# Routing the class token in the opening, and a new order of work on all engines, in a one-core image tower on Trainium2

## The chip, the core and the metric

The kernel runs on one core of one Trainium2 chip. The core has five engines with queues of their own: TensorE (PE: matrix products and transposes, its weight loads shown as PEld), VectorE (DVE), ScalarE (ACT), GpSimd (POOL) and SyncE (SP, which here only issues DMAs). They work in parallel and wait for each other on semaphores. The metric is the device time of one execution in microseconds (us). All data is fp32; `fp32r` is an fp32 format of TensorE with fewer bits, so a product that must be exact is made of three: high by high, high by low and low by high.

## What is computed

For each of 16 images of 256 tokens with 256 features: an attention-free mixing of tokens with a residual and a layer norm; one class token in front; a gated linear recurrence over the 257 tokens, added; and a mixture of experts (one shared, eight routed, the two best for each token), added. Cut to what matters:

```python
q, k, v = proj(Wq, bq), proj(Wk, bk), proj(Wv, bv)          # x: (16, 64, 256, 4)
ek = exp(k)
num, den = einsum('ts,nsd->ntd', ew, ek * v), einsum('ts,nsd->ntd', ew, ek)
h = layernorm((sigmoid(q) * num / den) @ out_w + out_b + flatten(x)) * ln_g + ln_b
h = concatenate([cls_tok of each image, h], axis=1)
u = layernorm(h)
r, i = sigmoid(u @ W_r + b_r), sigmoid(u @ W_i + b_i)
a = sigmoid(log_a) * r
hs = scan(h_s = a_s * h_{s-1} + (1 - a_s) * i_s * (u @ W_in + b_in)_s)
h = h + hs @ W_out + b_out
v = layernorm(h)
gate = top 2 of softmax(v @ Wr), scaled to sum 1
h = h + gelu(v @ Wfc_s + b) @ Wproj_s + b + sum_e gate_e * (gelu(v @ Wfc[e] + b) @ Wproj[e] + b)
```

The recurrence starts from zero with the class token, which is the same for all images. So its row is the same in all 16 outputs and is computed once.

## The kernel before

**Stages.** `mixer_tensor`, `mixer_scalar`, `mixer_vector`, `mixer_pool` and `mixer_sync` hold the program of the engines for the first stages; `experts_tensor` and its likes hold the rest. The mixer is a pipeline over 16 images with four in flight. In step t the projection and the sums over tokens work on image t, the layer norm, gates and recurrence on image t-1, its output and the second norm on image t-2, and routing and the shared expert on image t-3. Steps 0 to 3 are the opening, steps 4 to 15 a loop of pairs (`step`, twice), steps 16 to 18 the drain. Then come the eight routed experts, in blocks of 256 rows taken from per-expert lists `v_rows` in DRAM.

**Who sets the order.** Each engine's order is written out by hand as a list of calls with (t, parity). The calls with the same meaning on different engines meet through semaphores. Below, `name[n]` is the call's work on image n. On TensorE: `project0/1` (fp32 projection, L832), `sums0/1` (numerators and denominators, L925), `turn_y`, `turn_u`, `turn_v` (transposes, L839, all through the one buffer `ps_t`), `h_out` (L913), `gates0/1` and `input0/1` (split products, L748), `attention` (L898), `logits` (L994), `rank` (L879 to L883), `hidden` 0 to 7 (split product of the shared expert's first layer, L748) and `ffn_out` 0 to 7 (second layer, L764). On ScalarE: `exp0/1`, `copy_yt`, `copy_u`, `copy_v` (copies out of `ps_t`), `tanh0/1`, `gelu_j`, `high` (high half of the activation, L1293) and `share` (the tanh that gives the two scores' shares). On VectorE: `ekv0/1` (E, L1765), `ratio0/1` (reciprocal and product, L1772), `y_last` (L1864), `h_sum` (L1785 and statistics), `h_norm`, `u_stats`, `u_norm`, `u_low`, `gate_a` and `gate_b` (decay, recurrence input and scan, L1858), `v_sum`, `v_norm`, `v_low`, `low` (low half, L1593), `best` and `second` (the two best experts by small operations of 128x16, each waiting for the one before), `places` and `slots_out` (row numbers in the lists), `base_sum` (shared output plus residual, L1996 and L1999). On GpSimd: `rstd_h`, `rstd_u`, `rstd_v` (L517, L520), `affine` (L585, L587), `out_bias` (L598), `rows_out` (four scatters, L524), and the splits `low_first`, `low_second`, `next_low_first`, `next_low_second` of expert weights (L510, two instructions of 128x1024 each) and `next_weights` (six DMAs).

**The class token.** It goes through the mixer in the opening in `cls_` calls. Its routing stands in the drain: `cls_logits` (`cls_c` on TensorE: 8 small matmuls that turn the row into columns, then 4 for the logits), `cls_high` and `cls_share` on ScalarE, `cls_route` (`cls_c` on VectorE, 28 counted operations in a chain), `cls_d` (its count into `run`, the number of rows in each expert's list so far) and `cls_out` (two scatters). `run` is shared: what reads `ps_h` or `run` waits for `run_ready`, which also counts the class token from image 14 on. `CLS_AFTER`, `past_cls` say where it stands.

**Start of the experts.** After the drain TensorE makes the class token's shared output (24 matmuls, L1257), loads the eight ends of the experts' blocks from `bounds` into registers (`block_limits`, L1269), runs 8 matmuls with no use for their result (`WARM`, L1262), and transposes the first 256 rows (L1234). ScalarE and VectorE make `xh` and `xl` from them (L1572, L2246), for which the first hidden product waits.

## Time and profile before

| | |
|---|---|
| Median of 3 runs | 1000.52 us (1000.45 to 1001.65) |
| The profiled execution | 1000.1 us, its span 998.5 us |
| Mean granted clock of TensorE | 0.971 |
| Busy: TensorE, its weight loads | 941.2 us (94%), 879.6 us (88%) |
| Busy: VectorE, ScalarE, GpSimd | 676.5 us (68%), 458.8 us (46%), 380.1 us (38%) |
| DMA | 84.84 MB, mean 85 GB/s |

The time is the whole execution; the span runs from the first to the last instruction. Busy time of an engine is not work at its best rate: matmuls are pipelined, and TensorE's clock is granted at 2.4 GHz or at half of that. A view by stretches tells both: its columns are the stretch, its length, and for each engine the busy time with the number of instructions, then the granted clock, the DMA share and the rate. A view of waits names for whom an engine stood idle. In a timeline each row has its start, how long it took, the engine, the line, the operation, out<-in with shapes, the number of merged instructions, and in brackets the idle time before it and what ended it.

### The profile page before, as it was taken

The numbers are of one execution on the slowest core, as the hardware profiler recorded it, in microseconds if no ns is written. First come the engines' busy times: TensorE is split into PE (matmuls) and PEld (weight loads), VectorE is DVE, ScalarE is ACT, GpSimd is POOL, SyncE is SP. The second block draws the span as 40 slices with busy tenths as digits, with TensorE's granted clock in tenths as the row PEclk, the third lists the DMA queues.
The fourth block names the chain that finished last, engine by engine and source line by source line (L and its number), as shares of the span: only waits on it lengthen the run. The fifth ranks groups of instructions, "written<-read, shape, count | busy, mean of one in ns | idle before, by whom it ended". The sixth has DMA issues, their size and how long they took to land.

```text
span 998.5 us, 21487 instructions
## 1 busy us (share of the span) xinstructions
PE 941.2 (94%) x6801; PEld 879.6 (88%) x6801; DVE 676.5 (68%) x2092; ACT 458.8 (46%) x1132; POOL 380.1 (38%) x470
## 2 busy tenths in 40 slices
PE   6879999999999999999886999999999999999996
PEld 4667898888898888988786999999999999999995
DVE  3687878877888777788887365645656456554643
ACT  2214344444444434444332455555555555555553
POOL 5272533334324243233535334342423435342322
PEclk9989999999999999999999899999999999999998
DMA  9305111011110011100025727372463826474222
GB/s 271 134 18 168 43 43 37 17 32 42 42 42 16 26 42 42 42 21 11 33 95 195 202 47 204 55 216 43 101 157 50 215 47 145 117 174 92 43 43 32
DMA packets 49187, 84.84 MB, mean 85 GB/s; under 512 B 6415, under 2 KB 30881, under 8 KB 49154
## 3 DMA queue, kind: packets, MB, share of 16 engines
q0 software_dynamic: 31056, 57.46, 23.6%
q1 hardware_dynamic: 18098, 26.96, 9.2%
q8 instruction: 17, 0.28, 0.1%
q14 instruction: 16, 0.13, 0.0%
HBM read 55.34 MB, written 29.09 MB: 85 GB/s over the span
## 4 chain that ended last, share of the span: by engine, by line
PE 59%; issue 21%; POOL 9%; DVE 7%; ACT 1%; POOLq 1%; DMA 0%; DVEq 0%; SPq 0%; ACTq 0%
PE ps_nd L764 17%; PE ps_proj L748 13%; PE ps_ri L748 6%; PE ps_nd L925 6%; PE ps_proj L832 5%; POOL out L709 5%; PE ps_ip L748 4%; PE ps_h L913 2%; PE ps_t L839 2%; PE ps_ip L898 2%; PE ps_t L1234 1%; POOL v_rows L524 1%; DVE E L1765 1%; POOL rstd L520 1%; DVE yb L1999 1%
## 5 line engine op out<-in xcount | busy, mean ns | idle before, releaser
L1593 DVE TENSOR_TENSOR GL<-g_act,GH 128x256 fp32r<-128x256 f32 (+1 forms) x416 | 171.3, 425 | 166.4 <-ACT GH L1293 164.9
L1288 ACT ACTIVATE g_act<-ps_proj,fcb 128x256 f32<-128x256 f32 (+1 forms) x272 | 129.5, 476 | 277.9 <-PE ps_proj L748 253.4
L764 PE MATMUL ps_nd<-w2h,GH 128*128 128x256 f32 x832 | 240.6, 289 | 2.4 <-DVE GL L1593 2.2
L764 PE MATMUL ps_nd<-w2h,GL 128*128 128x256 f32 x832 | 233.8, 281 | 0.0
L764 PE MATMUL ps_nd<-w2l,GH 128*128 128x256 f32 x832 | 232.9, 280 | 0.0
L764 PEld LDWEIGHTS ps_nd<-w2h,GH 128*128 128x128 f32 x832 | 156.3, 188 | 6.9 <-issue 1.8
L1293 ACT CAST GH<-g_act 128x256 fp32r<-128x256 f32 (+1 forms) x416 | 161.0, 401 | 1.1
L764 PEld LDWEIGHTS ps_nd<-w2l,GH 128*128 128x128 f32 x832 | 157.0, 189 | 0.0
L764 PEld LDWEIGHTS ps_nd<-w2h,GL 128*128 128x128 f32 x832 | 156.4, 188 | 0.0
L748 PE MATMUL ps_proj<-xh,w1h 128*128 128x256 f32 (+1 forms) x544 | 126.8, 315 | 10.1 <-DVE E L1765 8.7
L709 POOL DMA_INDIRECT out<-yb,rows_to x72 | 115.6, 1605 | 16.7 <-issue 14.0
L748 PE MATMUL ps_proj<-xl,w1h 128*128 128x256 f32 (+1 forms) x544 | 111.8, 287 | 0.0
L748 PE MATMUL ps_proj<-xh,w1l 128*128 128x256 f32 (+1 forms) x544 | 111.3, 286 | 0.0
L748 PEld LDWEIGHTS ps_proj<-xh,w1h 128*128 128x128 f32 x544 | 86.7, 192 | 26.1 <-issue 14.3
L338 POOL TENSOR_TENSOR carrier_pool<-minus_half 1x1 f32<-1x1 f32 x48 | 10.9, 226 | 206.4 <-DVE slots L1987 113.9
L748 PEld LDWEIGHTS ps_proj<-xl,w1h 128*128 128x128 f32 x544 | 86.6, 194 | 0.0
L748 PEld LDWEIGHTS ps_proj<-xh,w1l 128*128 128x128 f32 x544 | 85.9, 193 | 0.0
L524 POOL DMA_INDIRECT v_rows<-v,slots x64 | 67.9, 1060 | 32.7 <-issue 16.6
L832 PE MATMUL ps_proj<-wproj,x 65*128 65x256 f32 x256 | 71.2, 425 | 6.8 <-DMA x<-x 6.2
L925 PE MATMUL ps_nd<-E,ewT 128*128 128x512 f32 x128 | 72.8, 702 | 2.8 <-DVE E L1765 2.8
L832 PEld LDWEIGHTS ps_proj<-wproj,x 65*128 65x128 f32 x256 | 64.1, 327 | 9.9 <-issue 7.9
L338 POOL TENSOR_TENSOR carrier_y<-minus_half 1x1 f32<-1x1 f32 x36 | 9.4, 261 | 162.8 <-DVE yb L2314 162.8
(266 smaller groups left out, 1829.9 us busy)
## 6 DMA issues: line engine op xcount, KB each, us to landing
R<-v_rows SPq DMA_DIRECT2D x37, 260.0 KB, 2.7
w1h<-fc_w POOLq DMA_DIRECT2D x9, 1024.0 KB
w2h<-pj_w POOLq DMA_DIRECT2D x9, 1024.0 KB
stage<-fc_w POOLq DMA_DIRECT2D x9, 1024.0 KB, 11.4
stage<-pj_w POOLq DMA_DIRECT2D x9, 1024.0 KB, 13.9
v_rows<-tail_rows SPq DMA_DIRECT2D x8, 520.0 KB, 4.5
x<-x SPq DMA_DIRECT2D x16, 256.0 KB, 3.5
out<-yb SPq DMA_DIRECT2D x16, 256.0 KB, 2.1
```

The costliest lines, as they stand in the source:

```text
L338: return pool.tensor_tensor(carrier[use][:], half, half, ALU.add)
L524: pool.indirect_dma_start(out=v_rows, out_offset=bass.IndirectOffsetOnAxis(ap=where_to, axis=0), in_=source, in_offset=None).then_inc(sema ...
L709: pool.indirect_dma_start(out=out, out_offset=bass.IndirectOffsetOnAxis(ap=rows_to[:, a:a + 1], axis=0), in_=yb[:, a, :], in_offset=None, ...
L748: last = pe.matmul(dst, w[a][:, k, cols], rhs, start=(q == 0), stop=(q == len(parts) - 1))
L764: last = pe.matmul(banks[a], g[:, j, a * P:(a + 1) * P], w[i][:, j, :], start=(j == 0 and q == 0), stop=(j == HT - 1 and q == 2))
L832: last = pe.matmul(ps_proj[:, h, :], head_view(par, lt, h), wproj[:, h, :], start=True, stop=True)
L839: last = pe.transpose(ps_t[:, f, lt * P:(lt + 1) * P], src[:, lt, f * P:(f + 1) * P], ident[:])
L898: last = pe.matmul(ps_ip[:, lt, :], HS[:, k, lt * P:(lt + 1) * P], wout_sb[:, k, :], start=(k == 0), stop=(k == FT - 1))
L925: last = pe.matmul(ps_nd[:, tt, :], ewT[:, s, tt * P:(tt + 1) * P], E[:, s, :], start=(s == 0), stop=(s == LT - 1))
L1288: act.activation(g_act[:, j % G_SLOTS, 0:width], banks[j % len(banks)][:, 0:width], ACT.Gelu_apprx_tanh, bias=fcb[i][:, j:j + 1]).then_inc ...
L1293: act.copy(GH[:, j, 0:width], g_act[:, j % G_SLOTS, 0:width]).then_inc(gh_done, 1)
L1593: dve.tensor_tensor(GL[:, j, 0:width], g_act[:, j % G_SLOTS, 0:width], GH[:, j, 0:width].bitcast(F32), ALU.subtract).then_inc(gl_done, 1)
```

## The change

**Class token.** `CLS_AFTER` goes from image 14 to 0: it is routed before image 0. Its calls are cut finer (`cls_cols`, `cls_logits`, `cls_count` on TensorE; `cls_halves`, `cls_route`, `cls_places`, `cls_run` on VectorE) and stand in the opening; the two scatters end GpSimd's opening. From there on all waits on `run_ready` and on the routing chain count it.

**Order.** The lists of TensorE, ScalarE, VectorE and GpSimd are new in the opening and the drain, and those of TensorE, ScalarE and VectorE in the loop's step. `low_first` moves ahead of `rstd_h[0]`, `low_second` ahead of the class token's rstd and `rstd_h[1]`, `next_weights` behind `rstd_v[1]`, `next_low_second` ahead of `rows_out[14]`. The projection and all other operations are what they were.

**Limits.** TensorE loads five limits (`AHEAD = 6`), transposes the first rows and then loads the other three; the 8 warm-up matmuls go. ScalarE loads its eight as before.

The core of the diff; in the lists only the step's are given whole, as they are after:

```diff
-        CLS_AFTER = NIMG - 2
-        CLS_STEP = CLS_AFTER + 2
+        CLS_AFTER = 0
         def past_cls(n, count):
-            return count if isinstance(n, int) and n >= CLS_AFTER else 0
+            return 0 if isinstance(n, int) and n < CLS_AFTER - 1 else count
...
             def cls_c():
                 pe.wait_ge(cls_dve, 9)
-                pe.wait_ge(run_ready, CLS_AFTER)
+                pe.wait_ge(hx_done, CLS_AFTER + 2)
                 columns(CV, ps_h[:, 0, :], 2).then_inc(cls_pe, 1)
+            def cls_scores():
...
             def logits(t, par):
                 if live(t - 3):
                     n = t - 3
-                    if isinstance(n, int) and n == CLS_AFTER:
-                        cls_d()
...
-            limits = block_limits(pe)
-            for _ in range(WARM):
-                pe.matmul(ps_t[:, 0, :], ones_r[:], W2H[0][:, 0, :], start=True, stop=True)
+            limits = [0] + block_limits(pe, 1, AHEAD)
             transpose_rows(0)
+            limits += block_limits(pe, AHEAD, NE + 1)
             pe.wait_ge(b_done, FT * NIMG)
...
+            def cls_rows():
+                count, chain = cls_chain(CLS_MASK)
                 dve.wait_ge(route_act, CLS_AFTER + 1)
-                dve.wait_ge(run_ready, CLS_AFTER)
-                dve.wait_ge(slots_ready, CLS_AFTER)
```

The steps of the loop, before and after:

```
TensorE before: turn_y project0 h_out attention project1 logits hidden0 sums0 hidden1 sums1 hidden2
  hidden3 turn_u hidden4 rank hidden5 gates0 turn_v hidden6 input0 gates1 input1 ffn_out0 ffn_out1
  hidden7 ffn_out2 ... ffn_out7
TensorE after:  turn_y project0 h_out attention project1 logits hidden0 hidden1 sums0 hidden2 hidden3
  hidden4 hidden5 turn_u hidden6 sums1 hidden7 gates0 input0 rank turn_v gates1 ffn_out0 ... ffn_out7
  input1
VectorE before: ekv0 h_sum h_norm ekv1 v_sum best u_stats second u_norm ratio0 u_low v_norm low0 low1
  ratio1 y_last low2 places low3 low4 low5 low6 slots_out v_low gate_a low7 gate_b base_sum
VectorE after:  ekv0 h_sum h_norm ekv1 v_sum best u_stats v_norm low0 u_norm low1 ratio0 u_low low2
  second low3 ratio1 y_last low4 places slots_out v_low low5 low6 low7 gate_a base_sum gate_b
```

The pieces of the opening and the drain of which the prediction speaks, after the change:

```
TensorE, opening: ... turn_u[1] cls_logits project1[3] turn_v[0] gates0[1] hidden0[0] turn_y[2] input0[1]
  cls_count h_out[2] hidden1[0] logits[0] ...
ScalarE, opening: ... copy_u[1] exp1[3] cls_share copy_v[0] copy_yt[2] gelu_j0[0] ...
VectorE, opening: ... u_low[1] v_norm[0] cls_route ekv1[3] v_low[0] y_last[2] cls_places cls_run h_sum[2]
  best[0] ...
GpSimd, opening:  low_first rstd_h[0] affine[0] rstd_u[0] out_bias[0] low_second cls_rstd rstd_h[1]
  affine[1] rstd_u[1] out_bias[1] rstd_v[0] rstd_h[2] affine[2] rstd_u[2] rstd_v[1] next_weights
  rows_out[0] out_bias[2] cls_out
TensorE, drain:   turn_y[15] hidden0[13] h_out[15] hidden1[13] attention[14] logits[13] ... ffn_out2[13]
  turn_u[15] ffn_out3[13] ... ffn_out7[13] hidden0[14] hidden1[14] logits[14] attention[15] ...
  hidden4[15] rank[15] ffn_out0[15] ...
VectorE, drain:   ... places[14] slots_out[14] base_sum[14] best[15] second[15] low0[15] places[15] ...
```

## Rows read from the trace of the kernel before

**Rows 1.** Busy time by stage: opening, loop, drain with experts' start, experts.
```profile
0.00:106.50 106.50, 85.31 (x415) 67.55 (x416) 70.54 (x175) 29.08 (x74) 46.49 (x69) 0.94 0.48 138
106.50:476.90 370.40, 361.69 (x2342) 325.71 (x2341) 298.67 (x970) 166.80 (x384) 136.98 (x173) 0.97 0.10 34
476.90:553.80 76.90, 59.91 (x449) 56.19 (x447) 59.93 (x211) 24.15 (x62) 32.63 (x30) 0.94 0.29 101
553.80:998.50 444.70, 434.31 (x3600) 430.11 (x3600) 247.39 (x740) 238.74 (x612) 163.95 (x199) 0.99 0.49 111
```

**Rows 2.** Timeline of TensorE: hidden0 of three steps in a row.
```profile
179.53 0.38 PE L748 MATMUL ps_proj<-xh,w1h 128*128 128x256 f32 x1 [0.68 <-DVE E L1765]
...
209.41 0.39 PE L748 MATMUL ps_proj<-xh,w1h 128*128 128x256 f32 x1 [0.68 <-DVE E L1765]
...
240.91 0.39 PE L748 MATMUL ps_proj<-xh,w1h 128*128 128x256 f32 x1 [0.68 <-DVE E L1765]
```

**Rows 3.** Waits of TensorE in the drain: total us, times, longest.
```profile
PE ps_h L994 <- DVE run L1761: 3.2, 1, 3.2
PE ps_h L994 <- issue: 2.7, 1, 2.7
PE ps_nd L764 <- DVE GL L1593: 1.6, 1, 1.6
...
PE ps_t L839 <- DVE U L1616: 1.0, 1, 1.0
```

**Rows 4.** Timeline in the drain: class token's columns, its chain's first and last operation.
```profile
498.11 1.05 PE L777 MATMUL ps_h<-ones_pp,CV 1*128 1x1 f32 x8
...
499.39 0.16 DVE L1724 TENSOR_TENSOR xl<-ps_h,xh 128x4 fp32r<-128x4 f32 x1
...
505.88 0.17 DVE L1756 CAST c_slots<-rslot 128x2 uint32<-128x2 f32 x1
```

**Rows 5.** Drain timeline of GpSimd and VectorE; then yb's durations (min/median/max ns).
```profile
477.62 4.67 POOL L510 TENSOR_TENSOR w1l<-stage,w1h 128x1024 fp32r<-128x1024 f32 x2
...
478.05 4.81 DVE L1999 TENSOR_TENSOR yb<-yb,h 128x512 f32<-128x512 f32 x1
...
L1999 DVE TENSOR_TENSOR yb<-yb,h x16: 691/691/5261, 110.1 to 541.0; 128x512 f32<-128x512 f32 x16
```

**Rows 6.** Loads of the limits by line (ns); then the timeline around them.
```profile
L1269 PEldq TENSOR_LOAD <-bounds x8: 295/308/724, 543.4 to 548.8; - x8
...
548.63 0.17 DVE L2241 COPY info<-R 128x8 f32<-128x8 f32 x1 [2.41 <-DMA R<-v_rows]
...
551.32 1.05 PE L1234 MATMUL ps_t<-ident,R 128*128 128x128 f32 x4
```

**Rows 7.** Busy time in a stretch at the experts' start, with the granted clock.
```profile
547.60:557.90 10.30, 7.05 (x31) 6.66 (x32) 2.12 (x9) 1.83 (x4) 0.37 (x2) 0.50 0.14 40
```

**Rows 8.** Opening: a weight load's issue and us to landing, rstd_h[0], v_norm[0].
```profile
15.20 0.96 POOL L486 DMA_DIRECT2D stage<-pj_w  x1
...
stage<-pj_w POOLq DMA_DIRECT2D x1, 1024.0 KB, 13.3
...
31.25 0.20 POOL L517 TENSOR_TENSOR ve<-mv,eps 128x2 f32<-128x2 f32 x1 [9.65 <-DVE mv L1613]
...
67.45 3.67 DVE L1616 TENSOR_SCALAR v<-h,mv,rstd 128x256 f32<-128x256 f32 x2
```

**Rows 9.** A step: chain pieces of sums and hidden; U, out_bias and turn_u.
```profile
457.39 1.72 PE ps_nd L925 x4
459.11 0.71 PE ps_proj L748 x6
...
184.85 0.73 DVE L1616 TENSOR_SCALAR U<-h,mv,rstd 128x256 f32<-128x256 f32 x2
185.66 1.28 POOL L598 TENSOR_TENSOR h<-h,bout_bc 128x512 f32<-128x512 f32 x1 [0.86 <-DVE U L1616]
185.90 0.27 PE L839 MATMUL ps_t<-ident,U 128*128 128x128 f32 x1
```

More of the change, by code:

```diff
@@ L1183, in mixer_tensor @@
             ffn_out(17, 1, 1)
+            turn_v(17, 1)
+            ffn_out(17, 1, 2)
+            hidden(17, 1, 7)
+            ffn_out(17, 1, 3)
             input0(17, 1)
[L1185 to L1196 removed]
@@ L2154, in mixer_vector @@
[L2154 to L2167 removed]
+            ratio0(17, 1)
+            v_low(16, 0)
+            low(16, 0, 7)
+            gate_a(16, 0)
+            gate_b(16, 0)
@@ new lines, in mixer_vector @@
+            base_sum(16, 0)
+            ratio1(17, 1)
+            y_last(17, 1)
+            low(17, 1, 0)
+            v_sum(17, 1)
+            best(17, 1)
+            low(17, 1, 1)
+            v_norm(17, 1)
+            gate_a(17, 1)
+            low(17, 1, 2)
+            h_sum(18, 0)
+            low(17, 1, 3)
+            ekv0(16, 0)
+            ratio0(18, 0)
+            v_sum(18, 0)
+            low(17, 1, 4)
+            second(17, 1)
+            h_norm(18, 0)
+            ekv1(16, 0)
```

512 lines of the change are left out of this document (251 added, 261 removed).

## The prediction

> **What bounds the kernel now.** I read three views in this order: the busy time by stage, what TensorE waited for in each stage, and then the timeline at the places where it waited. The stages say most [rows 1]: in the loop TensorE is busy 361.7 of 370.4 us and in the experts 434.3 of 444.7, so those two stages, 815 of 998.5 us, can hardly change. The opening (images filling the pipeline, 106.5 us) has 21.2 us in which TensorE is idle, the drain with the start of the experts (76.9 us) has 17.0. VectorE is busy 59.9 of these 76.9 us and 70.5 of 106.5, with long chains of small dependent operations between. So the change can win only in 183 us, and there what decides is when VectorE and GpSimd finish the item for which TensorE waits.
>
> In the loop each step has one idle piece of 0.68 us, in front of the first hidden product, which waits for the last E of the next image [rows 2]. Steps take 29.88 and 31.50 us in turn (from 179.53 to 209.41, then to 240.91): the longer ones hold a stretch at the lower clock. Nothing in the edit touches the chain project1, three ScalarE operations, E, on which the 0.68 us hang.
>
> **The drain, order and class token.** Its waits are in [rows 3]: 3.2 us until the class token's count is in `run`, 2.7 in front of the logits of image 13, 1.6 for GL and 1.0 for U.
> - Class token away: the 3.2 us are a pure wait, logits[14] behind `cls_d`, behind the VectorE chain that runs from 499.39 to 506.05 [rows 4]. The chain is 6.7 us long, of which about 6.0 busy. It goes, and so does its TensorE part (14 matmuls, some 1.5 us by the 1.05 us of eight of them [rows 4]). What is late next: hidden0[14] now stands first in that step and waits for v_low[14], which the new VectorE order has behind places and slots of image 13. I lay it out with the measured durations and find no stall there, because the 6.0 us that VectorE saves lie just before. Sum: -3.2 -1.5 = -4.7.
> - The 2.7 us: VectorE's yb sum, 0.69 us in the median, took 4.81 us because GpSimd ran its two weight splits (2.35 us each) at that time [rows 5]. The new step puts base_sum ahead of gate_b, so the sum now just escapes and the two scans of gate_b, with both inputs in SBUF, meet the splits. attention[14], moved ahead of logits[13], waits for these scans. I find the same stall, 0.8 us longer: +0.8.
> - The 1.6 us for GL have the same cause, a second 5.26 us yb sum [rows 5] beside the other half of the splits. That half moves ahead of image 14's sum: -1.6. The U wait: turn_u[15] goes behind three ffn parts: -1.0.
> - New waits: VectorE takes all of second[15] before low0[15], and rank[15] and ffn_out0[15] wait for them. I find 1.2 us: +1.2.
> - The drain holds one stretch at the lower clock, and I let the new one have one too: 0.
> Together -4.7 + 0.8 - 1.6 - 1.0 + 1.2 = -5.3.
>
> What the Trainium skill says bears on this: in "SBUF — State Buffer", section "SBUF: two separate sides", VectorE and GpSimd share a pair of ports as an exclusive lock, held for a whole instruction, and an operation of VectorE with two SBUF inputs asks for it. The 4.81 us agree with it. If the lock did not take the scans, the +0.8 above would be about -2.7; if it did, what I have stands.
>
> **Start of the experts.** TensorE starts its eight loads of limits between 543.4 and 548.8, one in 0.77 us with the check behind it, then runs 8 warm-up matmuls, and only then, at 551.32, the first transposes, although the rows have been there since 548.63 [rows 6]. The change loads five (to 547.2), transposes, and loads three more (2.3 us) while ScalarE and VectorE make xh and xl. So the transposes start at 548.7, hidden could follow 2.5 us later (551.32 to the 553.8 of [rows 1] is the same path) at 551.2, and the limits at about 549.5 + 2.3 + 0.2 = 552.0. The limits end last. Hidden starts at 552.0 rather than 553.8: -1.8. What the warm-up gave is not to be seen: the granted clock is at its lower level from 547.6 to 557.9 [rows 7], beyond the warm-up and four microseconds into the first block, which costs some 2 us now. Without it the rise may come up to 1 us of work later or at the same place; I take +0.5. Sum -1.3. ScalarE keeps its eight loads in one piece. If they end after the transposes its copy waits, under cover of TensorE's limits.
>
> **The opening.** Here things are added.
> - Class token: the chain of [rows 4], 6.0 us of VectorE, now runs between v_norm[0] and h_sum[2]. Its first half (up to the score difference) stands ahead of v_low[0], and copy_v[0] on ScalarE is queued behind cls_share, which waits for it. hidden0[0], the first product of the experts' part, waits for v_low[0], as do turn_v, the low parts and with them the end of the step. Against this, v_norm[0] took 3.67 us because it met a split [rows 8]; 0.7 is its normal length, and the splits are now done by then: -2.9. The TensorE part (1.5 us) lies in idle time.
> - Splits: low_first is now in front of rstd_h[0]. Its weights land at about 15.20 + 13.3 = 28.5 us; it takes 5 us, so rstd_h[0] starts at 33.6 instead of 31.25 [rows 8]. ratio0[1] and ratio1[1], two long reciprocals, fill VectorE in that time, and they were late before. low_second stands in front of the class token's rstd and rstd_h[1], beside y_last[1], which has two SBUF inputs: up to 2.5 us of turn_y[1].
> - Laid out to h_out[1] the new order is level with the old, with sums0[2] some 4 us sooner on TensorE, but VectorE's chain for image 0 eats that: v_low[0], two short steps behind v_norm[0]'s end at 71.12 now, comes about 1 us sooner. From there the second half of the class token's chain stands ahead of h_sum[2], and gate_b[1] is later. I get the end of the opening between 2 us sooner (y_last not caught, all the filled waits kept) and 6 us later (y_last caught, the clock low for the whole of it). The rows are nearer to the later end, since VectorE is busy two thirds of the time and gets 6 us more; with the level middle counted in: +1.0.
> - GpSimd: the six loads of next_weights pass rstd_h[2] to rstd_v[1], which is good for VectorE; the two scatters of the class token now stand in front of the loop's first rstd_h, and with the h chain the first E of the loop: +0.5.
>
> **The loop.** The same instructions in another order. Between hidden0 and turn_u TensorE had two sums (1.72 us each) and three hidden parts (0.71 each); it has one sum and five now [rows 9], so turn_u asks 0.3 us sooner. U was done at 185.58, turn_u ran at 185.90. VectorE's v_norm and low0 now stand in front of U where four small operations of second stood; GpSimd's rstd_u may lose 0.2 to 0.5 us to them at the ports. A stall of 0 to 0.3 us in the six faster steps, nothing in the slower. ratio1 comes later, but I find it done before ffn_out0 asks. gate_b gets input1 at the step's very end and has turn_y, project0 and h_out of the next step as cover; I find its scans 1 us ahead of attention, and whatever they lose of that cover attention would wait. +0.5. The number of slower steps, 7 of 12 in this execution, may be 6 to 8: plus or minus 1.6.
>
> **Sum.** -5.3 - 1.3 + 1.0 + 0.5 + 0.5 = -4.6. The profiled execution took 1000.1 us, of which 998.5 are its span; that makes 995.5. The median of the runs is 0.4 above it, so I give 995.9. The bounds of the parts: drain -11 (no scan stall, no low clock) to -1, start -2.5 to 0, opening and first step -3 to +7, loop -2 to +3.
>
> **Rivals.**
> 1. *The drain's wait moves.* v_low[14] and low1[14] come as late as the count did, because VectorE still has all its own work there (59.9 of 76.9 us [rows 1]); only the start's 1.3 and the matmuls' 1.5 us are kept. With +2.0 elsewhere and the median's 0.4: 999.7. For: VectorE is the fullest engine beside TensorE. Against: the 6 us that leave are its own.
> 2. *Slower, a lock in every step.* low1 now stands directly behind u_norm. GpSimd's out_bias, 1.28 us, starts 0.1 us after U is complete [rows 9]. If out_bias gets the ports first, low1 waits 1.3 us, ratio0 and u_low move with it and gates0 stalls: up to 1.0 us per step, 12 us, so 1007. It decides at the point where out_bias starts before low1; today VectorE goes on without a gap and GpSimd needs 0.1 us more, which speaks against it. By the page named above whichever starts first holds the pair, so it would give this time only with that order reversed.
> 3. *The opening is worth more than the drain.* hidden0[0] hangs on copy_v[0] behind the class token's chain; each microsecond by which v_norm[0] comes after 67 moves the loop. From 5 us on the gain is gone; with +9: 1003.
> 4. *Both halves win.* The filled waits of the opening survive and the drain does all that the layout allows: 988.
>
> **Chances.** Forecast 0.55 (own range 990 to 999), rival 1 0.14, rival 2 0.08, rival 3 0.10, rival 4 0.13. A measurement of this kernel tells about 0.2% (2 us) from no change. The forecast is nearly all beyond that (0.53 faster, 0.02 same), rival 4 too; rival 1 gives 0.04 faster and 0.10 same; rivals 2 and 3 0.16 slower and 0.02 same. That is 0.70, 0.14 and 0.16. Between 986 and 1003 lie the forecast, rival 1, two thirds of rival 4 and half of rival 3.
>
> **What would show it.** Of the profile after: no wait of TensorE for `run`; logits[14] within 2 us of hidden0[14]; a wait of 3 us in front of attention[14] behind stretched scans; first transposes within 0.2 us of the info copy, hidden 3.3 us later; steps of 29.9 and 31.5 in turn; turn_y[3] at 106 to 110. The prediction fails if the loop's steps are longer by over 0.3 us, if the opening ends after 112, or if TensorE's idle time in the drain stays above 6 us.

## The result, and the profile after

The changed kernel takes 1008.9 us in the median (1007.7 to 1009.7) against 1001.1 us for the kernel before on the same chip: ratio 1.0075, 95% interval 1.0058 to 1.0093. It is slower by 7.5 us, where 4.6 us less were forecast and the range ended at 1003. Its profiled execution has a span of 1006.1 us. Of the kernel after, the busy time by stage, with the columns of [rows 1]:

```profile
0.00:112.00 112.00, 90.49 (x429) 71.84 (x430) 73.81 (x211) 28.91 (x76) 46.23 (x70) 0.89 0.38 110
112.00:481.40 369.40, 359.07 (x2342) 326.21 (x2341) 298.71 (x963) 164.64 (x384) 146.90 (x174) 0.98 0.13 42
481.40:561.30 79.90, 57.83 (x428) 53.47 (x426) 57.40 (x181) 23.68 (x60) 30.11 (x28) 0.90 0.27 94
561.30:1006.10 444.80, 434.48 (x3600) 430.26 (x3600) 247.65 (x740) 238.81 (x612) 164.02 (x199) 0.99 0.49 111
```

Against [rows 1], the opening is 5.5 us longer, the loop 1.0 shorter, the drain with the start of the experts 3.0 longer, and the experts are the same. The forecast for these was +1.5 (first step included), +0.5, -6.6 and 0. So two stages carry the miss: 4 us in the opening and 9.6 in the drain with the start. The loop's -1.0 is the clock: TensorE is busy 2.6 us less for the same instructions (0.98 in place of 0.97), and idle 1.6 us more.

What TensorE waited for in the drain and the start (total us, times, longest), the answer to [rows 3]:

```profile
PE ps_t L1241 <- DMA R<-v_rows: 9.8, 1, 9.8
PE ps_ip L899 <- DVE HS L1871: 9.1, 2, 6.0
...
PE ps_nd L763 <- DVE GL L1599: 0.7, 2, 0.5
```

The wait for `run` is gone, as forecast, and so is the one for U; that for GL fell to 0.7. Two others are new: 9.1 us for the scans (of which 3.1 were forecast, in front of attention[14]) and 9.8 us for the first rows of the experts, ahead of L1241. The prediction has no term for the second 6.0 us of scans and none for the rows.

**The scans of image 15.** The timeline of the kernel after where GpSimd and VectorE run side by side, with TensorE's wait at the end:

```profile
509.79 7.15 DVE L1871 TENSOR_TENSOR_SCAN HS<-A,c_h,S 128x256 f32<-128x256 f32 x2
...
509.87 1.29 POOL L597 TENSOR_TENSOR h<-h,bout_bc 128x512 f32<-128x512 f32 x1
511.10 4.64 POOL L509 TENSOR_TENSOR w2l<-stage,w2h 128x1024 fp32r<-128x1024 f32 x2
...
517.00 3.78 PE L899 MATMUL ps_ip<-wout_sb,HS 128*128 128x256 f32 x8 [6.01 <-DVE HS L1871]
```

The durations of the two scans (ns, min/median/max, then the starts):

```profile
L1871 DVE TENSOR_TENSOR_SCAN HS<-A,c_h,S x2: 720/3613/6506, 509.8 to 516.2; 128x256 f32<-128x256 f32 x2
```

One scan takes 720 ns, the other 6506 ns. The long one is the first; its record starts 0.08 us before GpSimd's bias and it ends at 516.3, 0.6 us behind GpSimd's last operation. It waited through the bias and both parts of `next_low_second`.

**The tails.** Behind image 14's places SyncE writes eight empty blocks behind the lists of rows (`tails`: 520 KB each, they wait for `ends_ready`). The prediction does not name them. First the kernel before, then the kernel after:

```profile
515.60 0.17 DVE L1969 CAST ends_i<-run 128x8 int32<-128x8 f32 x1
...
518.92 11.74 SPq L404 DMA_DIRECT2D v_rows<-tail_rows  x8
```

```profile
531.63 0.17 DVE L1980 CAST ends_i<-run 128x8 int32<-128x8 f32 x1
...
532.79 12.10 SPq L403 DMA_DIRECT2D v_rows<-tail_rows  x8
...
540.52 0.17 DVE L1998 CAST slots<-rslot 128x4 uint32<-128x4 f32 x1
...
544.94 0.51 SPq L357 DMA_DIRECT2D out<-yb  x1
...
549.20 0.96 POOL L523 DMA_INDIRECT v_rows<-v,slots  x1 [11.41 <-DMA v_rows<-tail_rows]
...
549.65 0.76 DVE L2007 TENSOR_TENSOR yb<-ps_nd,pjb 128x256 f32<-128x256 f32 x2 [5.36 <-DMA out<-yb]
...
558.73 0.17 DVE L2264 COPY info<-R 128x8 f32<-128x8 f32 x1 [2.98 <-DMA R<-v_rows]
```

The cast that releases the tails comes 16.0 us later, since `rank[14]` now stands behind `ffn_out6[14]` in step 17. The eight issues take 12 us on SyncE. Two things hang on them. Image 15's slots are there at 540.5, but its first scatter waits until 549.20 for the tails to land, so the first rows are read only at 558.7. And the store of image 14 is queued on SyncE behind them (544.94), so the sum of image 15 stands until 549.65, with the experts' bounds behind it on VectorE.

### The profile page after: what moved, and what is told of

Read it like the earlier page. It is cut to its first block, busy times and chain, and to the rows that moved or that the text cites. A ratio compares the mean times of both kernels' runs of the same rounds, so it can differ in the third digit from the quotient of the medians.

```text
span 1006.1 us, 21465 instructions
## 1 busy us (share of the span) xinstructions
PE 941.9 (94%) x6793; PEld 881.8 (88%) x6793; DVE 677.6 (67%) x2092; ACT 456.1 (45%) x1132; POOL 387.3 (38%) x470
## 4 chain that ended last, share of the span: by engine, by line
PE 42%; issue 29%; POOL 18%; DVE 6%; ACT 2%; DMA 1%; SPq 1%; POOLq 1%; DVEq 0%; ACTq 0%
PE ps_nd L763 14%; PE ps_proj L747 8%; PE ps_ri L747 5%; POOL out L708 5%; PE ps_ip L747 4%; POOL v_rows L523 3%; POOL rstd L519 3%; PE ps_proj L833 3%; PE ps_nd L926 3%; PE ps_t L840 2%; POOL h L586 2%; POOL h L584 2%; PE ps_ip L899 1%; PE ps_h L914 1%; PE ps_t L1241 1%
## 5 line engine op out<-in xcount | busy, mean ns | idle before, releaser
L1299 ACT CAST GH<-g_act 128x256 fp32r<-128x256 f32 (+1 forms) x416 | 158.8, 399 | 0.2
L747 PE MATMUL ps_proj<-xl,w1h 128*128 128x256 f32 (+1 forms) x544 | 112.0, 288 | 0.0
L337 POOL TENSOR_TENSOR carrier_pool<-minus_half 1x1 f32<-1x1 f32 x48 | 10.9, 228 | 202.0 <-DVE slots L1998 110.5
L833 PE MATMUL ps_proj<-wproj,x 65*128 65x256 f32 x256 | 73.4, 434 | 11.7 <-DMA x<-x 6.3
L926 PE MATMUL ps_nd<-E,ewT 128*128 128x512 f32 x128 | 63.1, 621 | 1.6 <-DVE E L1778 1.6
```

Source lines behind the costliest of these rows:

```text
L337: return pool.tensor_tensor(carrier[use][:], half, half, ALU.add)
L747: last = pe.matmul(dst, w[a][:, k, cols], rhs, start=(q == 0), stop=(q == len(parts) - 1))
L833: last = pe.matmul(ps_proj[:, h, :], head_view(par, lt, h), wproj[:, h, :], start=True, stop=True)
L926: last = pe.matmul(ps_nd[:, tt, :], ewT[:, s, tt * P:(tt + 1) * P], E[:, s, :], start=(s == 0), stop=(s == LT - 1))
L1299: act.copy(GH[:, j, 0:width], g_act[:, j % G_SLOTS, 0:width]).then_inc(gh_done, 1)
```

## The experiments

Numbers of code lines in the rows are those of each run's own kernel. They differ a little from run to run: in the run with the half beside the low parts they are one higher than in the kernel after. An interval behind a ratio is at 95%. A difference between two runs carries both intervals, so it is known to about 2 us. `HS` is the result of the scans, `GL` the low half of a hidden activation, `rmask_z` the mask that `rank` reads. Loop start means the first transpose of `turn_y[3]` (106.5 before, 112.0 after).

### The drain

**Image 14 routed early.** The edit, on four engines:

```
PE:   hidden(17, 1, 4) + rank(17, 1)         (was behind ffn_out(17, 1, 6))
DVE:  gate_b(16, 0) + best(17, 1), second(17, 1)
      low(17, 1, 2) + places(17, 1)
ACT:  share(17, 1) + gelu_j(17, 1, 2)        (was behind high(17, 1, 6))
```

> The kernel after, with the routing of image 14 early in the drain again: best[14] and second[14] stand on VectorE right behind gate_b[15], rank[14] on TensorE behind hidden4[14], share[14] on ScalarE ahead of gelu2[14], places[14] on VectorE behind low2[14]. Nothing else is changed. Theory T (the tails): in the kernel after, the eight tail DMAs on SyncE are issued from 532.8 because places[14] stands late, and the first scatter of image 15's rows (549.20) and the sum of image 15 (549.65, behind the store of image 14, queued on SyncE behind the tails) wait for them. With places[14] at about 524 to 527 the tails are issued some 5 to 8 us earlier, rows_out[15] starts within 1.5 us of its slots (540.5), and the sum of image 15 follows the last matmul of its second projection; the first hidden layer of the experts then comes at 555 to 556 in place of 561.3: -5 to -6 us, median 1003 to 1004. Rival D (the drain, not its end, is what was lost: scans under the lock, order on TensorE): the start stays 10 us or more behind the class token's matmuls whatever the tails do, under 1.5 us gained. Rival W (the register loads or the missing warm-up hold the start): the same, under 1.5 us gained.

Measured: 1.0037 (1.0022 to 1.0052), -3.8 us against the kernel after, median 1004.4. Its trace:

```profile
528.46 0.17 DVE L1980 CAST ends_i<-run 128x8 int32<-128x8 f32 x1
...
545.54 0.96 POOL L523 DMA_INDIRECT v_rows<-v,slots  x1 [7.04 <-DMA v_rows<-tail_rows]
...
555.01 1.12 PE L1241 MATMUL ps_t<-ident,R 128*128 128x128 f32 x4 [5.26 <-DMA R<-v_rows]
```

The cast is 3.2 us earlier, the first scatter 3.7, the first transposes 3.7. They move together, as the theory has it, and both rivals, which allowed 1.5 us, fall. It is less than the 5 to 6 us expected, because the tails are released only 3.2 us earlier and not 5 to 8, and they still hold the scatter.

**The second half out of the scans.**

```
POOL:  affine(17, 1)
-      next_low_second(18, 0)
       ...
       rows_out(18, 0)
+      next_low_second(18, 0)
```

> The kernel after, with GpSimd's second half of expert 1's low weights (next_low_second, 4.64 us at 511.10) behind rows_out[15], not beside the scans of gate_b[15]. Theory L (the lock): the scans of gate_b[15] take 7.15 us because two GpSimd blocks, the bias of image 15 (1.3 us) and this half, run beside them; without the half they take 1.5 to 2.8 us, attention[15] waits 0.5 to 2 us in place of 6.01, and the drain up to there is 4 to 5 us shorter. The tails' chain starts from the same VectorE order, so it moves along: median 1003.5 to 1005.5. Rival T2 (the tails are bound elsewhere): the wait goes, but the gap ahead of the experts grows by as much and the time stays within 1 us of 1008.9.

Measured: 1.0025 (1.0012 to 1.0037), -5.0 us against the kernel after, median 1003.3.

```profile
509.89 2.55 DVE L1871 TENSOR_TENSOR_SCAN HS<-A,c_h,S 128x256 f32<-128x256 f32 x2
...
512.50 0.70 PE L899 MATMUL ps_ip<-wout_sb,HS 128*128 128x256 f32 x2 [1.40 <-DVE HS L1871]
```

The scans take 2.55 us and the wait 1.40 in place of 6.01. The cause of the 6.0 us is shown. TensorE's wait for the first rows is then 10.5 us in place of 9.8, so 0.7 of the gain goes into that wait and the rest stays.

**Both repairs.** The half now behind `rows_out(17, 1)`, rank, places and slots of image 14 a little earlier still.

> The kernel after with both repairs of its drain: image 14 routed early (best, second, rank, share, places and slots of image 14, so that the tails' DMAs start at about 522), and GpSimd's second half behind rows_out[14], out of the scans of gate_b[15]. Theory T+L: the two gains add up, for they lie one behind the other: drain -5 us from the scans (measured -5.4 when only the half was moved), and the start of the experts about 8 us behind the class token's matmuls in place of 12.3 (-4.5): the first hidden layer at 551 to 553, median 998.5 to 1000.5. The half's 4.6 us now lie beside the sum of image 14, which can cost TensorE up to 1.6 us at one GL. Rival D: only one of the two counts, median 1003 to 1005.

Measured: 1.0014 (1.0001 to 1.0026), median 1001.9; the first hidden layer at 555.4 in place of 561.3. That is 2.5 us better than image 14 early alone; against the half alone the gain of 1.1 us lies within the intervals. It is some 2 us short of what was expected, for a reason that the trace shows:

```profile
526.97 5.55 DVE L2010 TENSOR_TENSOR yb<-yb,h 128x512 f32<-128x512 f32 x1
527.26 4.70 POOL L509 TENSOR_TENSOR w2l<-stage,w2h 128x1024 fp32r<-128x1024 f32 x2
...
535.35 0.39 PE L880 MATMUL ps_h<-rmask_z,ones_r 128*128 128x24 f32 x1 [4.32 <-DVE rmask_z L1961]
```

The half met the sum of image 14, and behind that sum on VectorE stood `best[15]` and `second[15]`, for which TensorE waited.

**The half beside the low parts.** `next_low_second` behind `rstd_v(17, 1)` with a wait on `v_ready`, and the sum of image 14 behind `second(18, 0)`.

> The kernel after with image 14 routed early and the half of expert 1's low weights behind v_norm[15] (a wait on it), beside VectorE's low halves of the hidden layer, which have kept their 0.42 us each beside GpSimd; the sum of image 14 stands behind second[15]. In the run with both repairs TensorE waited 4.32 us for rank[15]'s mask, because the sum of image 14 (5.5 us beside the half, in place of 0.7) stood ahead of it on VectorE. Theory T+L: that wait goes, and with it 4 us: first hidden layer of the experts at 550.5 to 552.5, median 997 to 999. Rival: the lock only moves, onto slots[14] and the sum of image 14; under 2 us gained, median 1000 to 1002.

Measured: 0.9992 (0.9977 to 1.0008), -8.3 us against the kernel after, median 1000.5. The mask is no longer waited for, but only some 2 us were gained on the run before, where 4 were expected. The expectation was wrong in one point: the low parts do not keep their 0.42 us.

```profile
523.31 5.69 POOL L509 TENSOR_TENSOR w2l<-stage,w2h 128x1024 fp32r<-128x1024 f32 x2 [0.85 <-DVE v L1623]
...
524.94 4.68 DVE L1600 TENSOR_TENSOR GL<-g_act,GH 128x256 fp32r<-128x256 f32 x3 [0.71 <-ACT GH L1300]
```

Three of them took 4.68 us, and TensorE waited 1.5 us for GL at 529.3. The split and VectorE still hold each other up here, but TensorE's longest wait for it is 4.5 us shorter than on the scans.

**The old order in the drain**, on all four engines, without the class token's pieces, which stay in the opening.

> The kernel after, with the order of the drain on all four engines as in the kernel before, less the class token's pieces (they stay in the opening). This is the class token's move with the new opening, step and start, and no new drain. Theory T+L: the drain is before's 66.4 us less the 4.7 us of the class token (wait for run 3.2, its matmuls 1.5), and the start is before's less up to 1.8 us; with the opening's +5.45 and the loop's -0.94 that is 1000.1 + 5.5 - 0.9 - 4.7 - 1.3 = 998.7 profiled, median 998 to 1001. Rival O (the drain's new order is no worse than the old one, and what was lost is the opening and the clock): median 1007 to 1010 as after.

Measured: 1.0002 (0.9985 to 1.0019), median 1000.3. Undoing the drain's order alone takes back 7.3 us. So the new order there costs 7.3 us, where the prediction's terms for it add up to -0.6. The run before this one keeps the new order but routes image 14 early, moves the half and moves one sum, and it is level with this one (1000.5 against 1000.3). So those places account for all that the new order of the drain cost.

### The start of the experts and the step, alone

> The kernel before, with the limits of the experts' loops split around the first transposes and the eight warm-up matmuls gone, nothing else: one part of the change alone. The prediction's own term for it is -1.3 us (-1.8 for the loads, +0.5 for the clock): ratio 0.9987, median 999.0 to 1000.5. If the eight matmuls had kept the clock, the low stretch at 547.6 gets longer by 3.4 us and more, and the gain is gone: ratio 1.000 to 1.002.

The edit is the hunk of the change on `WARM`, `AHEAD` and `block_limits`, put into the kernel before. Measured: 0.9981 (0.9971 to 0.9991), -1.9 us.

```profile
550.61 0.17 DVE L2240 COPY info<-R 128x8 f32<-128x8 f32 x1 [2.27 <-DMA R<-v_rows]
...
550.63 1.11 PE L1234 MATMUL ps_t<-ident,R 128*128 128x128 f32 x4 [5.26 <-DMA R<-v_rows]
```

The transposes follow the info copy at once, where they came 2.7 us behind it in [rows 6]. The interval reaches from -0.9 to -2.9 us and so holds the -1.3 of the prediction.

> The kernel before with the new order of the loop's step on TensorE, ScalarE and VectorE and nothing else. The prediction's term for it is +0.5 us. Theory S (the steps are bound by TensorE's work and the turn_u stalls are under 0.2 us, the -0.94 of the loop is a low stretch of the clock more or less): ratio 0.9995 to 1.001, with the loop within 1 us of 370.4. Rival (the new step is faster by itself): 0.998 to 0.999, with the loop at 369.5 or less for the same number of low stretches.

The edit is the new `step` of TensorE, ScalarE and VectorE in the kernel before. Measured: 1.0011 (0.9999 to 1.0024), +1.1 us. Two steps in a row:

```profile
228.27:259.63 31.36, 30.68 (x197) 27.97 (x196) 24.91 (x81) 13.63 (x32) 11.76 (x14) 0.95 0.11 34
259.63:289.82 30.19, 29.34 (x198) 26.62 (x197) 24.39 (x80) 13.73 (x32) 11.77 (x14) 1.00 0.11 35
```

A step at full clock takes 30.19 us in place of 29.88 [rows 2], one with a stretch at the lower level 31.36 in place of 31.50. A pair takes 61.55 us in place of 61.38, so six pairs 1.0 us more. The interval still touches no change, and the loop as a whole took 369.5 us (370.4 before).

### The opening

**Two partial returns.** `cls_copy` behind `exp0(1, 1)` on ScalarE and both halves of expert 0's low weights back in their old places (first); `cls_gates` behind `turn_u(1, 1)` and `cls_scan` behind `u_low(1, 1)` (second).

> The kernel after, in whose opening the copy for the class token (cls_copy) stands on ScalarE behind exp0[1] again, and GpSimd's two halves of expert 0's low weights stand where the kernel before has them. Theory H (the heads of the queues): cls_copy at the head of ScalarE puts the first exponentials 1.6 us later and low_first holds rstd_h[0]; undone, the loop starts 1.5 to 2.5 us earlier than at 112.0: median 1006.5 to 1007.5. Rival G (the class token's gates and scan are the whole of the +5.45): loop start within 0.7 us of 112.0, median 1008 to 1009.5.

> The kernel after, in whose opening cls_gates stands on TensorE behind turn_u[0] and cls_scan on VectorE behind u_low[0] (in the kernel after they stand ahead of both). Theory G: cls_gates (3.7 us of TensorE ahead of turn_u[0]) and cls_scan, ahead of u_norm[0] on VectorE, put turn_u[0] at 45.7 in place of 38.8; with them behind, h_out[1] (54.1) comes 3 us earlier, and of that 2 to 3 us are left at the start of the loop: 109 to 110, median 1005.5 to 1007. Rival H (the heads of the queues on ScalarE and GpSimd): loop start within 0.7 us of 112.0. Rival C (the clock, 23.8 us of the opening at the lower level in place of 13.6, is the whole of it): the loop start follows the length of the low stretches and not the orders.

Measured: 1.0191 (1.0161 to 1.0220) and 1.0183 (1.0152 to 1.0214), with the loop starting at 120.4 and 121.8. Both made the opening 8 to 10 us longer. Theories H and G fall: moving back the pieces that looked late by the lists makes it worse, so what stands behind them in the new order seems to count on their place. Rival C (the clock) does not fall by these runs: TensorE's granted clock in their openings is 0.84 and 0.85, lower than the 0.89 of the kernel after.

**The new order without the class token's routing**, in the kernel before.

> The kernel before with the new order of the opening on all four engines, but without the class token's routing in it (columns, scores, count, route, places, run and rows stay in the drain, as before): the new order alone. Up to hidden0[0] the kernel after is only 1.0 us behind before (77.7 against 76.7); the other 4.4 us come between there and the loop, where VectorE has cls_places and cls_run ahead of h_sum[2] and TensorE cls_cols, cls_logits and cls_count. Theory K (the class token's chain on VectorE and TensorE is what costs): loop start at 106.5 to 108.5, median 999.5 to 1002. Rival Q (the order of the other pieces costs): loop start at 110 to 112, median 1004 to 1007.

Measured: 1.0038 (1.0024 to 1.0053), +3.8 us, loop start 110.55. Rival Q holds: the order costs this much without the class token's chain. The openings of this run, of the run with the half out of the scans, and of the kernel before with the class token in its old order (below):

```profile
0.00:110.55 110.55, 87.47 (x415) 69.05 (x416) 70.66 (x179) 28.70 (x74) 45.64 (x70) 0.91 0.39 111
```

```profile
0.00:110.64 110.64, 87.66 (x429) 68.92 (x430) 75.98 (x211) 28.99 (x76) 45.41 (x70) 0.92 0.38 111
```

```profile
0.00:108.37 108.37, 86.93 (x428) 68.66 (x429) 75.68 (x208) 29.10 (x76) 46.77 (x69) 0.94 0.48 136
```

How much of it is the clock? The kernel after has 90.49 us of TensorE busy at 0.89, and at first sight nearly its whole +5.5 us is busy time at the lower clock. But the second run here has the same opening at 0.92, with 2.8 us less busy, and its loop starts only 1.4 us earlier. The old order too has started at 104.2 with its clock at 0.92 (the run with the limits split and the half moved, in the last section of the experiments), 2.3 us ahead of [rows 1] at 0.94. So a lower clock alone does not make the loop start late. In most of the other runs the openings with the lowest clocks are the latest, and the runs do not tell which of the two brings the other.

The stretch from `hidden0[0]` to the loop start can be compared without the clock, for in these three kernels it is 1.00 there. In the kernel before, in the new order alone, and in the kernel after:

```profile
76.70:106.50 29.80, 27.75 (x195) 24.52 (x194) 25.50 (x70) 11.41 (x26) 5.80 (x8) 1.00 0.39 115
```

```profile
76.68:110.55 33.87, 29.57 (x205) 25.84 (x204) 25.64 (x73) 12.44 (x29) 10.12 (x15) 1.00 0.20 55
```

```profile
77.70:112.00 34.30, 29.59 (x207) 25.94 (x206) 27.56 (x86) 12.44 (x29) 10.15 (x15) 1.00 0.20 55
```

With the new order alone `hidden0[0]` comes at the same time as before, and all of the 4.1 us lie behind it: 1.8 are TensorE work that now comes later than `hidden0[0]` (205 instructions in place of 195), 2.2 are idle time (waits of 1.7 for U, 1.1 for the scans and 0.9 for Y).

**The class token with the old order.** The old lists of the opening with the class token's pieces put in, and the old drain without them. The new step, the split limits and the place of the two scatters (at the end of GpSimd's opening) stay as in the kernel after, so this is not the move alone.

> The kernel after with the old order of the opening, the class token's pieces put into it (columns behind sums1[2], scores behind turn_u[1], count behind hidden0[0], route behind v_low[0], places and run behind ekv1[3]), and the old drain without them: the class token's move with no new order around it. Theory K: its pieces cost the opening 3 to 5 us wherever they stand ahead of image 0's ranks, loop start at 109.5 to 111.5, median 998 to 1000. Rival Q: loop start at 106.5 to 108, median 995 to 997.5.

Measured: 1.0014 (1.0000 to 1.0028), loop start 108.4. The opening is better than expected, the time is not. The loop's first step took 34.8 us (32.1 before):

```profile
116.28 0.98 POOL L523 DMA_INDIRECT v_rows<-CV,c_slots  x1 [0.17 <-issue]
117.57 0.96 POOL L523 DMA_INDIRECT v_rows<-CV,c_slots  x1 [0.30 <-issue]
...
120.82 0.80 PE L747 MATMUL ps_proj<-xh,w1h 128*128 128x256 f32 x2 [3.76 <-DVE E L1778]
```

The class token's two scatters stand on GpSimd ahead of `rstd_h[3]`, and through it the first hidden product waits 3.76 us in place of 1.25. The run with the old drain differs from this one by the new opening only, and it took 1.0002: its loop starts 3.7 us later (112.1), but its loop is 3.6 us shorter (369.6 against 373.2). With the scatters where the change has them, the old order of the opening therefore gains nothing in the end.

> The drain of the last kernel with the opening of the one before it. The two lie a whole loop apart, so their gains should add: the time of the kernel after less what each of the two gained over it in its own stage. Theory K with T+L: loop start 110, first hidden layer 548.5 to 550.5, median 995 to 998. If one of the two gains fails here though it was seen alone, the clock's low stretches are what decides, and not the orders.

Measured: 1.0004 (0.9991 to 1.0016), median 1002.1, worse than expected: loop start 110.9, 2.5 us later than in the run with the same opening, and again the long first step (34.9 us). The first hidden layer comes at 556.7, where 548.5 to 550.5 were expected. The gains did not add.

**The scans of image 1 ahead of the reciprocals of image 3.** In the run with the order alone they start at 97.2, at 91.4 before.

```
DVE:  u_norm(3, 1) + gate_b(2, 0), ratio0(3, 1)
PE:   attention(3, 1) + ffn_out(3, 1, 0)
```

> The kernel after, in whose last step of the opening the scans of image 1 (gate_b[1]) stand behind u_norm[2] on VectorE, ahead of the reciprocals of image 3, and ffn_out0[0] behind attention[1] on TensorE; nothing else. Theory Z (the scans): attention[1] comes at 96 to 97 in place of 100.1, and the loop starts 2.5 to 3.5 us earlier, at 108.3 to 109.2: median 1005 to 1006.5. Rival (the reciprocals only come late in their stead, and TensorE waits for them): loop start within 1 us of 111.6, the mean of the six runs with this opening.

Measured: 1.0109 (1.0082 to 1.0135), loop start 116.2: worse by 3.4 us than the kernel after.

```profile
100.32 0.80 PE L747 MATMUL ps_ri<-UTH,gates_h 128*128 128x256 f32 x2 [5.98 <-DVE UTL L1819]
```

The edit left `u_low[2]` behind both reciprocals, and that is what TensorE then waited for. Theory Z isn't refuted in this way, but nothing supports it either.

> The kernel after with all that was found: image 14 routed early, the half behind v_norm[15], the sum of image 14 behind second[15], the scans of image 1 ahead of the reciprocals, and the class token's scatters ahead of rows_out[0]. Drain and start as in c5_drain_half (1000.5), opening -2.5 to -3.5 as in d1_scans, first step up to -0.5: median 996.5 to 998.5. If the scans in the opening are not the cause: 1000 to 1001.

Measured: 1.0005 (0.9989 to 1.0020), loop start 117.3, with the same 6.0 us for UTL. What the drain gives is there, and the opening takes it back.

**The two halves of the opening's order.**

> The kernel after, whose opening keeps its new order up to the exponentials and projection of image 3 and has the old order from there to the loop (scans of image 1, u_low[2], then the reciprocals of image 3 on VectorE, as in the kernel before), with the class token's pieces in their places. Theory Z2 (the order of the last step costs): loop start at 108 to 109.5 in place of 110.6 to 112.1, median 1005 to 1006.5. Rival Q2 (the head costs, and the last step only shows it): loop start within 1 us of 111.6, median 1008 to 1009.5.

> The kernel after with the old order of the opening's head up to the exponentials and projection of image 3, and its own new last step. Theory Z2: the head gives back 1 us at most, loop start at 110 to 111.5, median 1007 to 1009. Rival Q2: loop start at 107 to 109, median 1004 to 1006. If both runs come out at 111 or later, the two halves only fit together as they were, and neither order is good or bad by itself.

Measured: new head and old last step 1.0140 (1.0123 to 1.0157), loop start 113.7; old head and new last step 1.0078 (1.0061 to 1.0095), loop start 111.2. By the loop start neither half carries the loss by itself. With the class token in it, old with old gives 108.4 to 110.9 in three runs, new with new 110.6 to 112.1 in six, mixed 111.2 and 113.7. Without it the old order gives 104.2 to 106.5 in four runs, so one and the same opening moves by 2.3 us. The stretch from `hidden0[0]` to the loop start tells more. First new head and old last step, then old head and new last step:

```profile
82.10:113.73 31.63, 28.01 (x194) 24.73 (x195) 27.46 (x83) 12.32 (x29) 5.80 (x8) 1.00 0.18 66
```

```profile
76.20:111.15 34.95, 30.78 (x205) 27.45 (x206) 28.17 (x88) 12.43 (x29) 10.14 (x15) 0.95 0.19 54
```

The old last step takes 31.6 us there behind the new head and 31.5 to 33.1 behind its own, the new one 34 and more behind either. So the new last step is the longer one, as theory Z2 had it. But with the new head in front of the old last step `hidden0[0]` comes at 82.1, over 4 us later than in any run with one order throughout, and that hides it. Why these two do not fit together stays open.

### The class token's move alone

> The kernel before with the limits split (which gave 0.9981) and, besides, GpSimd's second half of expert 1's low weights behind v_norm[15] in place of behind rows_out[14]: it no longer lies beside the sum of image 14 (5.3 us there in place of 0.7), and TensorE's wait for GL at 531.9 (1.61 us) goes. Expected: ratio 0.9965, between 0.9955 and 0.9975, median 997 to 998.5. If the lock moves onto other work in the drain, 0.998 to 0.999.

Measured: 0.9972 (0.9962 to 0.9983), median 998.6, as expected. This is the run beside which the next one stands.

> The kernel before with the limits split and the half moved, as in the run beside it, and the class token routed in the opening with the old order everywhere: the move alone. Its scatters stand ahead of rows_out[0]. From the stages measured so far it costs the opening 1.8 to 4.4 us and saves the drain 2 to 3.5 us (the wait for run 3.2 and its matmuls 1.5, less 1.4 of a wait in step 16 that they had covered). Theory K: it is worth nothing, within 1.5 us of b3_before_half: ratio to the kernel before 0.995 to 0.998. The prediction's own sum (drain -4.7, opening about +0.5) would give 0.9925.

Measured: 0.9934 (0.9921 to 0.9948), median 994.5, the fastest of all. Between the two runs lies only the class token: 0.9934 / 0.9972 = 0.9962, 3.8 us, known to 1.7. The expectation that it is worth nothing is wrong. The two traces lie 6.1 us apart and not 3.8, for each is of the fastest execution of its run, and this one is far ahead of the other four (991.1 us, where they took 994.4 to 996.5). The stages of this run (opening, loop, drain, from the class token's shared output to the first hidden layer, experts):

```profile
0.00:108.82 108.82, 87.08 (x428) 68.64 (x429) 75.70 (x208) 29.10 (x76) 48.96 (x71) 0.94 0.47 138
108.82:477.55 368.73, 360.15 (x2342) 325.84 (x2341) 298.53 (x969) 166.77 (x384) 135.94 (x173) 0.97 0.11 35
477.55:538.11 60.56, 54.77 (x423) 51.11 (x421) 49.05 (x164) 23.27 (x59) 31.65 (x28) 1.00 0.31 113
538.11:545.15 7.04, 1.12 (x4) 0.72 (x4) 3.78 (x16) 0.59 (x1) 0.00 (x0) 0.77 0.33 94
545.15:989.50 444.35, 434.06 (x3600) 429.87 (x3600) 247.62 (x740) 238.74 (x612) 163.83 (x199) 0.99 0.49 111
```

The same stretches of the run beside it, up to the end of the drain:

```profile
0.00:104.22 104.22, 86.59 (x415) 68.47 (x416) 70.11 (x175) 28.97 (x74) 46.50 (x69) 0.92 0.50 142
104.22:474.50 370.28, 361.56 (x2342) 326.20 (x2341) 298.44 (x970) 166.79 (x384) 138.81 (x172) 0.97 0.10 34
474.50:543.61 69.11, 60.03 (x436) 56.41 (x434) 54.21 (x197) 23.49 (x61) 32.73 (x30) 0.93 0.28 101
```

The drain is 8.6 us shorter. TensorE is busy 5.3 us less in it: about 1.5 are the class token's matmuls, so 3.8 are the clock, 1.00 in place of 0.93. Idle time fell by 3.3 us, the wait for `run` (3.2 [rows 3]). So the 4.7 us that were forecast are there in this pair (3.3 + 1.5 = 4.8). In the run with the old drain, which has the new step, it was less: the wait for `run` is gone, but the one in front of the logits of image 13 grew from 2.7 to 4.1 us, and TensorE's idle time in the drain is 8.1 us against 9.4 before. The opening is 4.6 us longer, or 2.3 against [rows 1]; here the scatters stand ahead of `rows_out[0]`, in time in which GpSimd was idle, and the first step takes 31.9 us.

## Why the prediction was wrong

By the runs that did one part alone or undid it, in us of the ratio's difference:

| part | forecast | measured |
|---|---|---|
| class token moved | -3.2 (-4.7 drain, +1.5 opening and first step) | -3.8 |
| limits split, warm-up gone | -1.3 | -1.9 |
| step | +0.5 | +1.1 |
| new order of the drain | -0.6 (+0.8 -1.6 -1.0 +1.2) | +7.3 |
| new order of the opening | about 0 (level up to h_out[1]) | +3.8 |
| together | -4.6 | +6.5, where the change has +7.5 |

Each measured value is known to about 2 us. Two were measured in another setting than the change: the class token with its scatters ahead of `rows_out[0]`, and the new order of the opening without the class token. With the class token and the scatters as in the change, going back to the old order of the opening gained nothing, so the +3.8 is not a sure part of the +7.5.

**Right, by its own steps.** The wait for `run` went and nothing took its place on logits[14]. The stall of the scans ahead of attention[14] came as worked out, with a wait of 3.1 us. The transposes came 0.02 us behind the info copy. Hidden followed 2.5 us behind them and not 3.3: the last three limits do not end last. The step's and the limits' terms were right within what the runs can tell. The steps grew by 0.3 us at full clock and by less in pairs.

**Wrong: "where a stall goes, say what is late next", in the drain.** The prediction followed VectorE, TensorE and GpSimd and never asked what a moved `rank[14]` releases. It releases `places[14]`, that `ends_ready`, that eight DMAs with 12 us of issues on SyncE, and behind them both `rows_out[15]` and the store that frees `yb`. The term was missing, not mis-sized. The stretch from the class token's shared output to the first hidden layer is 1.8 us longer, where 1.3 less were forecast; the run with image 14 early took back 3.8.

**Wrong: the half moved "ahead of image 14's sum: -1.6".** The edit was costed at what it leaves (the sum) and not at what it meets. It met the scans of image 15, which was the very mechanism that the prediction had applied one image earlier. In addition the bias of image 15 now ran at the same time, so a single scan waited through three GpSimd operations. It cost 5.0 us by the run without it. The bound of -1 for the worst drain had no row behind it.

**Wrong: the opening.** The terms were laid out to h_out[1] and found level; there it was 5.3 us late. That was not what reached the loop, for `hidden0[0]` was only 1.0 us late (77.7 against 76.7). The step that failed is the one behind it: for the stretch to the loop start the prediction had no sum, only a bracket (2 us sooner to 6 us later), from which the level middle took it to +1.0. There every run with the new last step takes 34 us or more, in place of 29.8 in the kernel before and 31.5 to 33.1 with the class token in the old order. That the bracket held the result has no working behind it, and is in part luck. The class token's pieces, on which rival 3 rested, are a part of it: with them in the old order the loop starts 1.9 to 4.4 us later than in [rows 1], and 1.9 to 6.7 later than in the four runs with the old opening. Why the new order of the opening costs what it does is shown only down to its last step.

**Rivals.** 3 had the sign of the whole, but its cause, an opening longer by 9 us that eats the drain's gain, and its 1003 were not: the opening grew by 5.5, and the drain had no gain to eat. 1 named the right stage, though not the way: TensorE's idle time there did not just stay (17.0 us), it became 22.1. 2 fell: the steps have no new stall above 0.3 us. 4 was never near, but a kernel that leaves the old orders in place and moves the class token alone gives the time that was forecast, 994.5.

The prediction's own signs of failure were "the opening ends after 112" (111.99) and "TensorE's idle time in the drain stays above 6 us". The second is what happened: it was 10.9 us from 481.4 to the end of the class token's shared output (67.5 us with 56.7 busy).

## What to carry to other kernels

When an instruction is moved, follow every semaphore it sets to the last engine, the DMA-issuing ones included, and look at what is queued there behind the wait: here a block of eight DMA issues started 16 us later, and starting it 3 us earlier took back 3.8 us. A long GpSimd operation beside VectorE was paid for at every place where it was tried here: list what VectorE runs at the new place before taking credit for the old one. And a large reordering should be tried stage by stage: here the one structural edit was worth 3.8 us, the small one 1.9, and the three new orders around them, each measured by itself, lost 12.

## What was not expected of the hardware

- **A VectorE operation can wait through several GpSimd operations in a row.** A scan of 0.72 us took 6.51 beside one bias and two splits, and the sum of image 14 5.55 in place of 0.69 beside two splits (4.70 together). GpSimd's records follow each other there without a gap, and VectorE does not get in between. The 4.81 us of [rows 5], in which the prediction saw the Trainium skill confirmed, are a wait through two splits as well (4.67). It is not always so: beside the low parts one of them took 1.84 us and the next 2.58, each ending 0.2 to 0.3 us behind one of the two splits, so there VectorE did get in between. What decides it stays open. By the Trainium skill, "SBUF — State Buffer", section "SBUF: two separate sides", the pair of ports is held for one whole instruction. One split alone is 2.35 us [rows 5], so one instruction would hold VectorE no longer than that. The traces show waits of two and three instructions added up; the measurement decides.
- **The clock in the drain gave as much as the wait itself in one pair of traces.** With the wait for `run` gone TensorE's granted clock in the drain was 1.00, where it was 0.93 in the run that differs by the class token alone and 0.97 in the kernel before. Between the two runs that is 3.8 us of busy time. The drain's clock is known for one execution of each, the fastest of its run. But over the whole kernel all five executions have a mean granted clock of 0.971 to 0.976, and all eight of the other run 0.964 to 0.967. That the wait is what took the clock down was not tried by itself.
